# Perceiver block on one core: transposes of six context chunks and of the tail's weights moved from TensorE to the DMA, with GpSimd splitting and joining 16-bit halves

## The reference, cut to what matters

```python
q = (Q @ Wq.T + bq)...; k = (K @ Wk.T + bk)...; v = (V @ Wv.T + bv)...     # K = V = ctx_1024
scores = jnp.einsum('bhqd,bhkd->bhqk', q, k) / jnp.sqrt(HEAD_DIM) + mask
out = jnp.einsum('bhqk,bhkd->bhqd', jax.nn.softmax(scores, axis=-1), v)
...
x = x + _L0_xattn_ref(_layernorm(x), ctx_1024, ctx_1024, mask, Wq, bq, Wk, bk, Wv, bv, Wo, bo)
x = x + _L0_attn_ref(_layernorm(x), W_in, W_out, Wp, bp, alpha_log, delta_bias, log_gamma)
x = x + _L0_ffn_ref(_layernorm(x), w1, b1, w2, b2)
```

## Time and profile before

| | us |
|---|---|
| median of 3 runs | 291.2 (290.73 to 292.55) |
| the profiled execution's own time | 291.72 |
| its span in the profile | 289.9 |

### The profile page before, as it was taken

One profiled execution on the slowest core, in us unless ns is written; L12 is line 12 of the kernel. 1 busy time (PEld: TensorE's weight loads), 2 busy tenths in 40 slices (PEclk: granted clock), 3 DMA queues, 4 the chain that ended last, 5 costly groups with the idle time before them and its releaser, 6 DMA issues.

```text
span 289.9 us, 9826 instructions
## 1 busy us (share of the span) xinstructions
PE 264.6 (91%) x3991; PEld 191.7 (66%) x3991; DVE 223.1 (77%) x407; ACT 210.1 (72%) x441; POOL 101.1 (35%) x225
## 2 busy tenths in 40 slices
PE   8699789999999999999999999999999997841975
PEld 7376457676767676676777777777777664631965
DVE  4776878887878999887888898889889941539871
ACT  3575358888788888888888888888887785298032
POOL 5366765634444333333444454411121120100220
PEclk9999869999999999999999999999999999885699
DMA  6896935887532324242333322222222000000001
GB/s 196 293 312 179 290 94 154 241 210 202 165 115 75 119 66 120 77 137 80 118 108 102 119 66 66 67 80 84 70 84 77 2 3 2 1 0 0 0 2 38
DMA packets 21081, 30.55 MB, mean 105 GB/s; under 512 B 4272, under 2 KB 15052, under 8 KB 20908
## 3 DMA queue, kind: packets, MB, share of 16 engines
q1 hardware_dynamic: 17708, 28.00, 31.9%
q0 software_dynamic: 624, 1.06, 1.4%
q10 hardware_dynamic: 2704, 0.85, 1.2%
HBM read 22.43 MB, written 7.47 MB: 103 GB/s over the span
## 4 chain that ended last, share of the span: by engine, by line
PE 81%; DVE 8%; issue 4%; ACT 3%; DMA 2%; POOL 1%; ACTq 0%; POOLq 0%; DVEq 0%
PE ps L494 24%; PE ps L477 15%; PE ps L458 11%; PE ps L587 5%; PE ps L353 4%; PE ps L505 4%; PE ps L548 4%; PE ps L540 3%; PE ps L369 3%; PE ps L347 2%; PE ps L364 2%; DMA x_sb<-in_x_dram 2%; DVE pmax L1305 2%; PE ps L772 1%; ACT probs L877 1%
## 5 line engine op out<-in xcount | busy, mean ns | idle before, releaser
L1305 DVE TENSOR_REDUCE pmax<-ps 128x2 f32<-128x1024 f32 x128 | 156.1, 1224 | 28.8 <-PE ps L458 28.0
L877 ACT ACTIVATE probs<-ps 128x512 f32<-128x512 f32 x256 | 139.0, 595 | 19.9 <-PE ps L477 17.6
L477 PE MATMUL ps<-q_max,k_rows 59*128 59x128 bf16 x1024 | 82.4, 219 | 0.5 <-ACT probs L877 0.2
L494 PE MATMUL ps<-probs,v_all 128*9 128x128 f32 x2048 | 80.8, 276 | 0.7 <-ACT probs L877 0.7
L458 PE MATMUL ps<-k_rows,q_all 56*128 56x512 bf16 x256 | 78.7, 388 | 2.2 <-DVE pmax L1305 2.0
L477 PEld LDWEIGHTS ps<-q_max,k_rows 59*128 59x128 bf16 x1024 | 55.9, 94 | 5.2 <-ACT probs L877 3.1
L494 PEld LDWEIGHTS ps<-probs,v_all 128*9 128x9 f32 x2048 | 43.4, 90 | 14.9 <-ACT probs L877 1.0
L1114 POOL CAST max_cols<-negmax 128x2 bf16<-128x2 f32 x32 | 6.2, 193 | 119.6 <-DVE negmax L1311 119.6
L458 PEld LDWEIGHTS ps<-k_rows,q_all 56*128 56x128 bf16 x256 | 23.2, 94 | 21.3 <-issue 11.3
L347 PE MATMUL ps<-ones 128*128 128x128 f32 x86 | 15.0, 352 | 11.1 <-ACT k_parts L1003 10.1
L347 PEld LDWEIGHTS ps<-ones 128*128 128x128 f32 x86 | 14.5, 265 | 11.5 <-ACT k_parts L1003 10.5
(11 more groups left out here) (186 smaller groups left out, 330.0 us busy)
## 6 DMA issues: line engine op xcount, KB each, us to landing
k_rows<-k_parts_dram SPq DMA_DIRECT2D x59, 192.0 KB
k_parts_dram<-k_parts SPq DMA_DIRECT2D x16, 384.0 KB, 3.7
ctx_buf<-in_ctx_dram SPq DMA_DIRECT2D x16, 256.0 KB, 6.0
k_rows<-k_parts_dram SPq DMA_DIRECT2D x59, 32.0 KB
mask_sb<-in_mask_1x1xSxS_ff_dram SPq DMA_DIRECT2D x1, 1024.0 KB, 8.7
q_all<-q_rows_dram SPq DMA_DIRECT2D x2, 336.0 KB
k_rows<-k_parts_dram POOLq DMA_DIRECT2D x3, 192.0 KB, 3.8
q_rows_dram<-q_parts SPq DMA_DIRECT2D x2, 288.0 KB, 3.7
```

The lines of the kernel that those rows point to most:

```text
L477: t = pe.matmul(dst, k_rows[rows, i % 4, at:at + P], q_max[rows, i % 2, :], start=not masked, stop=True, skip_group_check=masked)
L494: t = pe.matmul(ps[at:at + HEAD_COLS, 6, 0:P], v_all[:, KT * (i // PAIRS) + 4 * c + j, first + HEAD_COLS * h: first + HEAD_COLS * h + HEAD ...
L877: act.activation(probs[:, u % CHUNKS, h, :], ps[:, 4 + h, :], ACT.Exp).then_inc(probs_ready, 1)
L1305: dve.tensor_reduce(pmax[:, i % 2, :, c], ps[:, bank:bank + 2, :], AX.X, ALU.max).then_inc(pmax_ready, 1)
```

## The change

Chunks 10 to 15 (`TURNED_FIRST` = 10) and all tail weights no longer go through TensorE. GpSimd copies a chunk's fp32 words as two 16-bit planes to a free part of `k_parts` (`part_ctx`, `part_weights`, `part_mlp`), SyncE issues one DMA transpose of all planes (`turn_planes`), and GpSimd joins the halves again in `ctxT`, `wT`, `w1T` or `w2T` (`join_ctx`, `join_weights`, `join_mlp`). In GpSimd's loop the part of the next chunk and the join of the present one stand in odd `i`, behind `split_max` and `split_k`. SyncE waits for the planes before it issues the transpose, and load requests of later pairs stand behind it. TensorE waits for `late_ctxT_ready` at place 2, ahead of the key projection, and before the tail for all joined weights.

```diff
+        TURNED_FIRST = FIRST + 2
+        TURNED_CTX = ALL_CHUNKS - TURNED_FIRST
...
+        def part_space(a, first, blocks):
+            return k_parts[:, a, first:first + P * blocks].bitcast(U16)
...
+        def planes(space):
+            return space.rearrange("p (j h n) -> p j h n", h=2, n=P)
...
+        ctx_planes, ctx_turn = part_space(2, 0, 8), part_space(2, 8 * P, 8)
+        w_planes, w_turn = part_space(2, KEYS, 12), part_space(0, 2 * KEYS, 12)
+        mlp_planes, mlp_turn = part_space(0, KEYS, 16), part_space(1, KEYS, 16)
...
+            def turn_planes(src, dst):
+                sp.dma_start(dst.rearrange("d (j n) -> d j n", n=P), src, transpose=True
+                             ).then_inc(once("planes_turned"), 16)
...
@@ (SyncE, in the loop over i, behind load_pair(i) and load_ctx)
+                n = FIRST + (i - 1) // 2
+                if i % 2 == 1 and TURNED_FIRST <= n < ALL_CHUNKS:
+                    sp.wait_ge(once("planes_ready"), n - TURNED_FIRST + 1)
+                    wait(sp, once("late_ctxT_ready"), n - TURNED_FIRST)
+                    turn_planes(ctx_planes, ctx_turn)
+                if i == 22:
+                    sp.wait_ge(once("planes_ready"), TURNED_CTX + 1)
+                    turn_planes(w_planes, w_turn)
+                elif i == 26:
+                    sp.wait_ge(once("planes_ready"), TURNED_CTX + 3)
+                    turn_planes(mlp_planes, mlp_turn)
...
@@ (TensorE, side_prep)
                 if at == 0:
-                    wait(pe, v_half_ready, 2 * m)
-                    if n == ALL_CHUNKS - 1:
-                        pe.wait_ge(pow_ready, 1)
-                        pe.wait_ge(once("gram_ready"), 1)
-                    turn_ctx(7, n)
+                    if n < TURNED_FIRST:
+                        wait(pe, v_half_ready, 2 * m)
+                        turn_ctx(7, n)
...
                 elif at in (2, 3):
                     if at == 2:
+                        if n >= TURNED_FIRST:
+                            pe.wait_ge(once("late_ctxT_ready"), n - TURNED_FIRST + 1)
                         side_taken(i)
...
@@ (TensorE, side_squares)
-                elif at == 6 and m in (0, 1, 3, 4):
+                elif at == 6 and m == 1:
                     side_taken(i)
-                    if m == 0:
-                        pe.wait_ge(ld["w"], 32)
-                        turn_weights(0, 4)
-                    elif m == 1:
-                        turn_vectors()
-                        turn_weights(4, 2)
-                    else:
-                        turn_binary(m - 3)
+                    turn_vectors()
...
@@ (GpSimd)
+            def to_planes(space, nat, s):
+                gp.tensor_copy(planes(space), nat.bitcast(U16).rearrange("p (j n h) -> p j h n", h=2, n=P)).then_inc(s, 1)
...
+            def from_planes(dst, space, s):
+                gp.tensor_copy(dst.bitcast(U16).rearrange("p (j n h) -> p j h n", h=2, n=P), planes(space)).then_inc(s, 1)
...
+            def part_ctx(n):
+                c = n - TURNED_FIRST
+                gp.wait_ge(ctx_loaded[n % CTX_SLOTS], 16 * (n // CTX_SLOTS) + 16)
+                wait(gp, once("planes_turned"), 16 * c)
+                to_planes(ctx_planes, ctx_buf[:, n % CTX_SLOTS, :, :].rearrange("p j d -> p (j d)"),
+                          once("planes_ready"))
...
+            def join_ctx(n):
+                c, m = n - TURNED_FIRST, n - EARLY - FIRST
+                gp.wait_ge(once("planes_turned"), 16 * c + 16)
+                gp.wait_ge(v_done, FIRST + 2 * m + 2 if m >= 0 else n - EARLY + 1)
+                from_planes(ctxT[:, n % EARLY, :], ctx_turn, once("late_ctxT_ready"))
...
@@ (GpSimd, in the loop over i, behind split_max(i) and split_k)
+                n = FIRST + (i + 1) // 2
+                if i % 2 == 1 and TURNED_FIRST <= n < ALL_CHUNKS:
+                    part_ctx(n)
+                n = FIRST + (i - 1) // 2
+                if i % 2 == 1 and TURNED_FIRST <= n < ALL_CHUNKS:
+                    join_ctx(n)
+                if i == 19:
+                    part_weights()
+                elif i == 22:
+                    join_weights()
+                elif i in (24, 25):
+                    part_mlp(i - 24)
+                elif i in (27, 28):
+                    join_mlp(i - 27)
```

More of the change, by code:

```diff
@@ L28 @@
 I32 = mybir.dt.int32
+U16 = mybir.dt.uint16
 ALU = mybir.AluOpType
@@ L267, in load_ctx @@
             def load_ctx(n):
-                wait(sp, ctx_turned, n - CTX_SLOTS + 1)
+                if n - CTX_SLOTS < TURNED_FIRST:
+                    wait(sp, ctx_turned, n - CTX_SLOTS + 1)
+                else:
+                    sp.wait_ge(once("planes_ready"), n - CTX_SLOTS - TURNED_FIRST + 1)
                 b, c = divmod(n, CHUNKS)
@@ L525, in side_prep @@
                 if at == 0:
-                    wait(pe, v_half_ready, 2 * m)
-                    if n == ALL_CHUNKS - 1:
-                        pe.wait_ge(pow_ready, 1)
-                        pe.wait_ge(once("gram_ready"), 1)
-                    turn_ctx(7, n)
-                elif at == 1:
-                    pe.wait_ge(ctxT_ready, n + 1)
+                    if n < TURNED_FIRST:
+                        wait(pe, v_half_ready, 2 * m)
+                        turn_ctx(7, n)
+                elif at == 1:
+                    if n < TURNED_FIRST:
+                        pe.wait_ge(ctxT_ready, n + 1)
+                    else:
+                        wait(pe, v_half_ready, 2 * m)
+                        if n == ALL_CHUNKS - 1:
+                            pe.wait_ge(pow_ready, 1)
+                            pe.wait_ge(once("gram_ready"), 1)
                     side_turns(i)
@@ L565, in turn_vectors @@
                 pe.wait_ge(ld["vec"], 16 * 5)
[L566 to L577, removed]
+                pe.transpose(ps[:, 7, 3 * P:3 * P + VECS], vec_nat[:, :], ident[0:VECS, 0:VECS]
+                             ).then_inc(once("vec_turned"), 1)
             def sum_norms(norms):
@@ L730, in finish @@
                     turn_half(h, o_nat, once("oN_turned"))
+                pe.wait_ge(once("wT_ready"), 3)
                 for h in range(2):
@@ L834, in _ @@
             act.wait_ge(once("kqv_turned"), 1)
-            copy(kvT[:, 0, :], ps[:, 2, 0:P], once("vec_ready"))
+            act.activation(kvT[:, 0, :], ps[:, 2, 0:P], ACT.Copy)
             copy(vec[:, 0:2], ps[:, 2, 3 * P:3 * P + 2], once("kT_ready"))
@@ L886, in side_prep @@
                 if at == 0:
-                    act.wait_ge(v_done, FIRST + 2 * m)
-                    copy_ctx(7, n)
+                    if n < TURNED_FIRST:
+                        act.wait_ge(v_done, FIRST + 2 * m)
+                        copy_ctx(7, n)
                 elif at in (2, 3):
@@ L920, in side_squares @@
                     take_square(SQ_PERIOD * m + (0, 0, 1, 2, 3)[at])
-                elif at == 6 and m == 0:
-                    act.wait_ge(once("w_turned"), 1)
-                    copy(wT[:, 0:4, :].rearrange("p a d -> p (a d)"), ps[:, 7, :], once("wT_ready"))
                 elif at == 6 and m == 1:
[L925 to L933, removed]
+                    act.wait_ge(once("vec_turned"), 1)
+                    copy(vec[:, 2:VECS], ps[:, 7, 3 * P + 2:3 * P + VECS], once("vec_ready"))
             for g in range(UNITS):
@@ L1095, in binarise, with part_weights, join_weights, part_mlp @@
                     gp.tensor_tensor(flat(w_bin, sl), flat(w_bin, sl), nat, ALU.add).then_inc(once("w_bin_ready"), 1)
+            def to_planes(space, nat, s):
[13 more added lines that the diff above has]
+                from_planes(ctxT[:, n % EARLY, :], ctx_turn, once("late_ctxT_ready"))
+            def part_weights():
+                gp.wait_ge(ld["w"], 32)
+                gp.wait_ge(ld["ssm"], 32)
+                to_planes(w_planes, w_nat[:, :, :].rearrange("p a d -> p (a d)"), once("planes_ready"))
+            def join_weights():
+                gp.wait_ge(once("planes_turned"), 16 * TURNED_CTX + 16)
+                from_planes(wT[:, :, :].rearrange("p a d -> p (a d)"), w_turn, once("wT_ready"))
+            def part_mlp(half):
+                gp.wait_ge(once("w_bin_ready"), 2)
+                to_planes(mlp_planes[:, 2 * HID * half:2 * HID * half + 2 * HID],
+                          flat(w_bin, slice(HB * half, HB * half + HB)), once("planes_ready"))
+            def join_mlp(half):
+                gp.wait_ge(once("planes_turned"), 16 * TURNED_CTX + 32)
+                from_planes((w1T, w2T)[half][:, :, :].rearrange("p a d -> p (a d)"),
+                            mlp_turn[:, 2 * HID * half:2 * HID * half + 2 * HID], once("wT_ready"))
             for n in range(EARLY):
@@ L1393, in _ @@
                        ).then_inc(once("first_step_ready"), 1)
-            dve.wait_ge(once("wT_ready"), 2)
+            dve.wait_ge(once("vec_ready"), 1)
             dve.tensor_tensor(sv[:, 5:6], vec[:, BP0:BP0 + 1], vec[:, DBIAS:DBIAS + 1], ALU.add
```

6 lines of the change are left out of this document (2 added, 4 removed).

## The result

The changed kernel takes 309.21 us (median of 4 runs, 307.11 to 309.55) beside 290.97 us (4 runs, 290.18 to 292.55) of the kernel before on the same chip: **1.064 times as long, 95% interval 1.059 to 1.069**, that is 18.2 us slower. The forecast was 301.2 us in a range of 292 to 322. A time here is the median of all executions, while a ratio and its interval leave out those over 1.5% above the fastest of their kernel. The profiled execution took 309.41 us, its span is 307.6 us, 17.7 more than before.

The account below looks back on a forecast made before the run. TensorE, busy 91% with 81% of the chain of waits, was taken to bound the kernel. 7.35 (joins) + 0.4 (pair 6) + 3.3 (pair 27) - 1.05 (weights) = +10.0 us, giving 301.2 us, range 292 to 322.

Parts of the forecast that it names:

- The chunks' join: TensorE waits for GpSimd's join before the key projection: 1.41 us in each of chunks 10 to 14, 0.30 in 15.
- The clock: Granted clock of 0.50 in units 16 to 63 would mean waits cost more than their length; left out of the sum.
- Pair 27: Its loads stand behind the perceptron weights' transpose on SyncE, so TensorE waits in unit 100: +3.3 us (1.9 to 4.7).
- The weights' transpose at i = 22 and the joins in turns 22, 27 and 28 cost nothing: Pairs there last 6.5 us, split_max is first in each turn and the sums stay below that: no cost.
- +0.4 at pair 6: Pair 6's loads, behind the first transpose on SyncE, land at 64.7, needed at 64.29: +0.4 us.
- The weights' gain: TensorE without weight transposes saves 0.35 us in each of rounds 0, 3 and 4, nothing in round 1: 1.05 us.
- Slow transposes: Rival: issue plus queueing of DMA transposes over 3.4 us; 340 us at 7.7 us, about 317 at 5; chance 0.15.
- Slow and cheap copies: Two rivals on GpSimd's copies: 1.94 us each, 313 us, chance 0.10; 0.61 us each, about 296, chance 0.10.
- Faster: Rival: the join is no last wait; 287.5 us, or 289.4 with 1.9 us of pair 27 against it; chance 0.06.

Follow-up runs that it names:

- filled_wait: Changed kernel with ten unused matmuls put ahead of TensorE's wait for the joined chunk: 308.24 us, ratio 1.060 to the kernel before.
- mlp_turn_after_load: Changed kernel with the perceptron weights' transpose issued in SyncE's turn 27, behind the loads of pair 27: 302.85 us, ratio 1.038 to the kernel before.
- weight_join_earlier: Changed kernel with join_weights in GpSimd's turn 21 in place of 22: 307.4 us, ratio 1.054 to the kernel before.
- all_moved: Changed kernel with join, then part, right behind split_max, perceptron weights' transpose in SyncE's turn 27, weights' join in turn 21: 288.52 us, ratio 0.992.
- join_before_part: Changed kernel with the join ahead of the part in GpSimd's turn: 301.95 us, runs too scattered for an interval.
- from_chunk_11: all_moved with chunk 10 left to TensorE, chunks 11 to 15 by DMA: 287.55 us, ratio 0.991 to the kernel before.
- weights_alone: Kernel before with only the weights turned by DMA (transpose in turn 27, join in turn 21), all chunks on TensorE: 289.5 us, ratio 0.995.

## Why the forecast was too small

Direction and order of size were right, the sum was +10.0 us and the measured difference +18.2. Step by step:

**The chunks' join: right in size, with two errors that cancelled.** Chunks 10 to 14 start their key projection 5.09 to 5.30 us after the first `pv` (forecast 5.2 to 5.4), chunk 15 after 3.98 (4.2). The forecast had the join end 5.23 us after the first `pv`; in chunk 13 it is 116.18 + 1.31 - 112.26 = 5.23. That the sum agrees to the last digit is luck: the join takes 1.32 us and not 1.03, but the rows of GpSimd overlap by 0.04 to 0.06 us where I had put gaps of 0.08. The chunks without half clock or late loads cost 1.48 and 1.42 us (forecast 1.41), chunk 15 cost 0.44 (0.30). Units 0 and 1 take 2.64 us in chunks 12 to 14, better than the 2.81, so a chunk relieved of its transposes gives 0.62 us and not 0.45; behind the wait for the join it makes no difference. The part took 1.03 us as computed from the rows. The Trainium skill's GPSIMD Engine Reference, § 3.1, with its 1.8 cycles an element, would have an estimated 1.54 us for either copy; the part is under it by a third, and the join, which writes every second 16-bit element, lies between.

**The clock: left out, 3 us in the chunks and 2 in unit 99.** The forecast named the sign that would show it and put no number to it. The half clock came after two of the four waits of 1.9 to 2.03 us in chunks 11 to 14, not after the 1.54 us of chunk 10, and cost 1.5 us each time; it came after the wait of 4.33 us too, where the three units lost 11.36 - 4.97 - 4.33 = 2.1 us. filled_wait and mlp_turn_after_load take the one and the other away. Why some of the chunks and not others stays open: the waits have the same length, and mlp_turn_after_load and weight_join_earlier lost the clock after three of their four. A wait of 1.70 us for pair 7 in all_moved was followed by half clock, one of 1.78 us for pair 6 in join_before_part was not.

**Pair 27: right mechanism, mis-sized.** Forecast +3.3, measured 4.33 of wait. The planes were ready as predicted: 12.8 us after the forecast's 198.9, as all of TensorE's units are. The 9 us that the forecast had to spare before the change run from the loads' issue; less the 5.0 that they take, 4 were to spare, which enters no sum. The issue took 2.76 us in place of 1.0, and the loads landed 5.6 us after their first issue, not 6.4. With the clock's 2.1 this place cost 6.4 us, as mlp_turn_after_load gives back.

**"The weights' transpose at i = 22 and the joins in turns 22, 27 and 28 cost nothing": wrong for turn 22.** The forecast priced the pair's length and not what comes behind the join on GpSimd. `binarise` moved by 1.9 us, onto VectorE's sum of squares, for 1.1 us. weight_join_earlier shows it.

**The loads in the busy stretch: +0.4 at pair 6.** In the change's profile pair 6 cost 0.14 and pair 7 0.54 us, 0.7 in all; other profiles have up to 2.7 us and half clock there. The forecast treated pair 6 alone and as fixed.

**The weights' gain: right.** Rounds 0, 1, 3 and, without unit 99, 4 gave 0.36, 0.21, 0.33 and 0.35, together 1.25 us for 1.05; round 1, to which the forecast gave nothing, is among them.

**The rivals.** Slow transposes: refuted. (Their price at 5 us was added up wrongly: the sum's own terms give about 320 us, not 317.) An issue takes 1.28 to 1.35 us for a chunk, and half of them land within 3.3 us, as the trace lists the transposes:

```profile
L305 SPq DMA_TRANSPOSE k_parts<-k_parts x8: 1279/1292/2760, 59.2 to 211.8; - x8
...
DMA to landing us min/median/max: 3.1/3.3/6.0
```

Slow and cheap copies: refuted, the price is 1.03 and 1.32 us, by the same view:

```profile
L1110 POOL COPY k_parts<-ctx_buf x6: 1027/1034/1038, 58.1 to 131.3; 128x1024 uint16<-128x1024 uint16 x6
...
L1113 POOL COPY ctxT<-k_parts x6: 1309/1318/1381, 70.3 to 145.8; 128x1024 uint16<-128x1024 uint16 x6
```

"Faster": not this kernel, but its price of 287.5 us, had the join been no last wait, is about what all_moved and from_chunk_11 reach, 288.5 and 287.6. They don't reach it by its sum, though: in the profile of all_moved chunks 11, 12 and 14 gain 0.62 us each, chunks 13 and 15 lose 0.38 and 0.09, and chunk 10 loses 2.66 by pair 7; the squares give 1.4, and the rest of its shorter span lies ahead of unit 16 and in the tail. In the profile of from_chunk_11 chunks 10 to 15 give 1.4 us and the squares 1.4, 2.9 in all beside the 3.75 of that price.

## What to carry to other kernels

An engine at 35% load can still be the last to arrive. Before work is handed to it, write down what stands ahead of that work in its queue within the window, in this kernel three long instructions that could all wait, and put what another engine waits for right behind the wait that releases the turn. A DMA that waits for data goes behind the loads that don't, and the time that its issue holds the queue counts too, here 1.3 to 2.8 us. Price a wait on TensorE with what can follow it: of the 18 us here some 5 were instructions at half clock after waits. Filling the waits of the chunks kept the clock up and cost about as much as it gave; removing the wait gave both.

## What the runs showed of the hardware

GpSimd copies 1024 16-bit elements a partition in 1.03 us when it reads them with a stride of two and in 1.32 us when it writes them so; 1536 take 1.46 and 1.91 us. In the changed kernel SyncE is held for 1.28 to 1.35 us by the issue of a DMA transpose of 128 x 1024 16-bit elements, for 2.59 us by that of 128 x 1536 and for 2.76 us by that of 128 x 2048, while an ordinary load's first DMA takes 0.78. This isn't a fixed price by size: the last took from 1.89 us (weights_alone) to 3.08 us (filled_wait) in other profiles, and the first one 2.43 us in all_moved. A VectorE instruction with two SBUF operands took 1.35 us for its 0.28 under a GpSimd instruction with two SBUF operands, and each of the two slowed sums ended 0.15 us after the GpSimd instruction beside it. One with a single SBUF operand took 1.57 us under GpSimd's 16-bit copies, 0.84 under a cast and 0.41 with GpSimd idle. After waits of 1.9 to 2.03 us TensorE's granted clock fell to 1.2 GHz in 8 of 12 cases, at a cost of 1.5 us each.
